# Selective scan on VectorE and GpSimd: decays of GpSimd's units in SBUF instead of PSUM, and later loads of delta

## The chip, the cores and the metric

The kernel runs on one core of a Trainium2 chip. The metric is the device time of one execution in microseconds (us). Three executions of the kernel before took 2348.87, 2349.60 and 2352.06 us; the median is 2349.6 us. In this text VectorE is DVE, GpSimd is POOL, ScalarE is ACT, TensorE is PE, and SP is the engine whose queue starts most of the DMAs, as in the profile.

## What is computed

The reference is one block of a vision model on an input of 4 x 32 x 32 x 384: a convolutional selective-scan layer, then a linear attention layer and a mixture of 8 experts. The change touches the scan alone. Cut to what matters:

```python
def step(h, inp):                       # over L = 1024 positions
    u_t, d_t, B_t, C_t = inp
    dA = jnp.exp(d_t[..., None] * As)   # the decay
    h = h * dA + (d_t * u_t)[..., None] * B_t[:, :, None, :]
    y = jnp.einsum('bkcn,bkn->bkc', h, C_t)
    return (h, y)
```

There are K = 4 directions, 192 channels and N = 16 states for each of 4 images. Two images and 64 channels of each fill the 128 partitions, and a pair of directions that are each other's reversal is taken in one tile.

## The kernel before, in words

The scan stage has NQ = 12 tiles of UN = 32 units; a unit is one state of one direction, 128 partitions x 1024 positions in f32, and the first 16 units of a tile (a half) run forward, the last 16 backward. For every unit five things are done:

- **decay**: ACT computes exp(a x delta) (line 762), and **C copy**: ACT copies the spread row of C from PSUM to SBUF (line 767);
- **input**: delta x u times B. Two units of three are DVE's: PE spreads the row of B over the partitions into a PSUM slot (`B_PS`, two slots; `spread`, line 1040), and DVE multiplies it in place (`input_of`, line 1496). Every third unit (u = 2, 5, ..., 29: `POOL_UNITS`, 10 of a tile) is POOL's: SP loads the row of B, broadcast, from DRAM into a ring of five SBUF buffers `xin` (`b_row`, line 424), and POOL multiplies it there (`make_input`, line 529);
- **scan**: DVE's tensor_tensor_scan of the decay `f` and the input `x` into a ring of eight SBUF buffers `hst` (`scan`, line 1513);
- **read-out**: POOL multiplies two units' `hst` by their C in one instruction of 2048 columns (`read_outs`, line 546);
- **Y**: PE adds the read-outs of a tile in PSUM with an identity matrix (`add_y`, line 1056), LAG = 5 units behind.

Where the operands of a scan lie: a DVE unit's decay is in SBUF (`decay`, two buffers taken in turn) and its input is in PSUM. A POOL unit's decay is written by ACT into the PSUM slot `B_PS[u % 2]`, and its input `xin` is in SBUF. The two PSUM slots are so shared by all 32 units of a tile by the parity of u. A slot or a buffer may be refilled when the scan of its last holder is done: PE waits at line 1075 for the scan of unit U-2, ACT at line 760 for the scan of `held`. The semaphore `sc_ok` counts finished scans and starts at 2.

The order on each engine is written out by hand. DVE goes in groups of three units (line 1517): the inputs of the two DVE units, then three scans, the POOL unit's last. POOL goes in pairs: before the read-out of units u and u+1 it makes the inputs of u+4 and u+5, if they are its own, so its order over six units is input, read-out, read-out, input, read-out. `read_outs` waits for the scans and the C copies of its pair (lines 543 and 544). PE does for each unit the B spread (DVE units), the C spread and a Y add of an earlier unit. SP walks over the units too (line 433): `b_row` of a POOL unit waits for the scan of the unit whose `xin` buffer it takes, five POOL units or 15 units back; and where U % 16 is `FETCH_AT` = 5, from the second half on, SP waits until the whole previous half is scanned (line 437) and then loads delta and delta x u for the half after this one (`load_delta`, lines 395 and 396). What stands behind that wait in SP's queue, the rows of B among it, waits too.

Of the kernel before, what the change touches and what calls it, by code (L numbers as in the profile page):

```python
# [13 lines left out]
B, HW, C, DI, N, R, K = 4, 32, 384, 192, 16, 24, 4  # L14
S = HW * HW
T = B * S
P = 128
CT = C // P
H2 = P // 2
J = DI // H2  # L20
NP = B // 2
# [6 lines left out]
UN = 2 * N  # L28
HALF = S // 2
HALVES = 2 * OJ  # L30
FETCH_AT = 5
RING = 8
DRING = 2
HRING = 8
# [3 lines left out]
XRING = 5  # L38
# [4 lines left out]
MADE = 4  # L43
# [42 lines left out]
def pool_units(u):  # L86
    return u // GROUP


POOL_UNITS = list(range(GROUP - 1, UN, GROUP))  # L90
# [19 lines left out]
    return k, j, p * OJ + o * J + j, dr  # L110


def decay_slot(u):
    return (u - pool_units(u)) % DRING


def decay_before(u):

    vec = [v for v in range(-UN, UN) if v % UN not in POOL_UNITS]
    return vec[vec.index(u) - DRING]  # L120


assert len(POOL_UNITS) % XRING == 0


# [22 lines left out]
def hybrid_block_kernel(nc, a, out):  # L148
    with ExitStack() as ctx:
        def sem(name):  # L150
            return ctx.enter_context(nc.semaphore(name))
# [10 lines left out]
        COLS = 53200  # L162
# [47 lines left out]
        rs = Region(arena, BCD, COLS)  # L210
        xin, decay = rs.take(XRING, S), rs.take(DRING, S)
        c_sb, hst = rs.take(RING, S), rs.take(HRING, S)
        d_diag = Region(arena, COLS - P, COLS).take(P)


# [46 lines left out]
        def pair_of_banks(b):  # L262
            return ps[:, b:b + 2, :].rearrange("p b c -> p (b c)")
# [6 lines left out]
        B_PS = [pair_of_banks(0), pair_of_banks(2)]  # L270
# [24 lines left out]
        ab_ok, dm_st = sem("abs_ready"), [sem(f"delta_stored{i}") for i in range(MADE)]  # L295
# [6 lines left out]
        b_ok, c_ok, c_free, dec_ok = (sem(n) for n in ("b_spread", "c_spread", "c_copied", "decay_ready"))  # L302
        p1_ok, sc_ok, p2_ok, ya_ok, yev_ok = (sem(n) for n in ("input_ready", "scanned", "readout_ready", "y_added", "y_evacuated"))
# [32 lines left out]
        def settled(eng):  # L336


            eng.sem_inc(passed, 1)
# [3 lines left out]
        def _(sp):  # L343
# [50 lines left out]
            def load_delta(q, dr):  # L394
                sp.dma_start(dlt[:, dr], dl_dram[q * 2 + dr]).then_inc(dl_ld[dr], 16)
                sp.dma_start(dux[:, dr], du_dram[q * 2 + dr]).then_inc(du_ld[dr], 16)
# [36 lines left out]
            for U in range(NQ * UN):  # L433
                if U % N == FETCH_AT and N <= U < (2 * NQ - 1) * N:

                    half = U // N + 1
                    sp.wait_ge(sc_ok, U - FETCH_AT + 2)
                    load_delta(half // 2, half % 2)
# [180 lines left out]
        def _(act):  # L619
# [118 lines left out]
            def skip_weights(q):  # L738
                nc.scalar.activation(d_diag, ident, ACT.Identity, scale=d_sum[:, q % OJ, :]).then_inc(diag_ok, 1)

            def evacuate_y(q):
                act.wait_ge(ya_ok, q * UN + (UN + HRING))
                nc.scalar.activation(xy[:, q, :], Y_PS, ACT.Copy).then_inc(yev_ok, 1)

            def units(q, first, last):
                for u in range(UN):
                    dr, n = divmod(u, N)
                    U = q * UN + u
                    if n == 0:

                        act.wait_ge(dl_ld[dr], q * 16 + 16)

                    if u == LAG and not first:
                        evacuate_y(q - 1)
                        skip_weights(q)

                    held = u - 2 if u in POOL_UNITS else decay_before(u)
                    dst = B_PS[u % 2] if u in POOL_UNITS else decay[:, decay_slot(u)]
                    if not (first and held < 0):
                        act.wait_ge(sc_ok, q * UN + (held + 3))  # L760
                        settled(act)
                    nc.scalar.activation(dst, dlt[:, dr], ACT.Exp,  # L762
                                         scale=a_neg[:, q % OJ, dr, n:n + 1]).then_inc(dec_ok, 1)
                    act.wait_ge(c_ok, U + 1)

                    act.wait_ge(p2_ok, U + 1)
                    nc.scalar.activation(c_sb[:, u % RING], C_PS, ACT.Copy).then_inc(c_free, 1)  # L767
# [5 lines left out]
            act.wait_ge(setup, 2)  # L773
            skip_weights(0)
            units(0, True, False)
            with nc.scalar.Fori(1, NQ - 1) as q:
                units(q, False, False)
            units(NQ - 1, False, True)
            evacuate_y(NQ - 1)

# [132 lines left out]
        def _(pe):  # L913
# [122 lines left out]
            def spread(q, u, m, dst):  # L1036

                dr, n = divmod(u, N)
                for h in range(2):
                    mm = pe.matmul(dst[:, h * 512:(h + 1) * 512], sel_lhs[0:BR, n],  # L1040
                                   bc[0:BR, q % OJ // J, dr, m, h * 512:(h + 1) * 512], start=True, stop=True)
                return mm
# [17 lines left out]
            def add_trailing_y(q, u, first):  # L1060
                if u >= LAG:
                    add_y(q, u - LAG)
                elif not first:
                    add_y(q - 1, UN - LAG + u)

            def tile_steps(q, first, last):
                if not first and not last:
                    pe.wait_ge(bc_ld, 16 * ((q + 1) // J + 1))
                for u in range(UN):
                    dr, n = divmod(u, N)  # L1070
                    U = q * UN + u

                    at = u % GROUP
                    if u not in POOL_UNITS:
                        pe.wait_ge(sc_ok, U + 1)
                        spread(q, u, 0, B_PS[u % 2]).then_inc(b_ok, 1)
                    if at == 1:
                        add_trailing_y(q, u - 1, first)
                    pe.wait_ge(c_free, U + 1)
                    spread(q, u, 1, C_PS).then_inc(c_ok, 1)  # L1080
                    if at:
                        add_trailing_y(q, u, first)
# [6 lines left out]
            pe.wait_ge(rows_ok, K * NP)  # L1089
            pe.wait_ge(dtev_ok, NP * HALVES)  # L1090
            tile_steps(0, True, False)
            with nc.tensor.Fori(1, NQ - 1) as q:
                tile_steps(q, False, False)
            tile_steps(NQ - 1, False, True)
            for u in range(UN - LAG, UN):
                add_y(NQ - 1, u)
# [233 lines left out]
        def _(dve):  # L1330
# [156 lines left out]


            def input_of(q, u):
                dr, x = u // N, B_PS[u % 2]  # L1490
                seen = q * VEC_UNITS + (u - pool_units(u) + 1)
                if u % N == 0:

                    dve.wait_ge(du_ld[dr], q * 16 + 16)
                dve.wait_ge(b_ok, seen)
                nc.vector.tensor_tensor(x, x, dux[:, dr], ALU.mult).then_inc(p1_ok, 1)  # L1496

            def scan(q, u):
                dr, U = u // N, q * UN + u
                h, slot = hst[:, u % HRING], B_PS[u % 2]  # L1500
                if u in POOL_UNITS:
                    f, x = slot, xin[:, pool_units(u) % XRING]

                    dve.wait_ge(in_ok, q * len(POOL_UNITS) + (pool_units(u) + 1))
                else:
                    f, x = decay[:, decay_slot(u)], slot

                    dve.wait_ge(p1_ok, q * VEC_UNITS + (u - pool_units(u) + 1))
                dve.wait_ge(dec_ok, U + 1)
                dve.wait_ge(ya_ok, U + 1)  # L1510
                if dr:
                    h, f, x = h[:, ::-1], f[:, ::-1], x[:, ::-1]
                nc.vector.tensor_tensor_scan(h, f, x, 0.0, ALU.mult, ALU.add).then_inc(sc_ok, 1)  # L1513

            def scans(q):

                for g in range(0, UN, GROUP):
                    units = range(g, min(g + GROUP, UN))
                    for u in units:
                        if u not in POOL_UNITS:  # L1520
                            input_of(q, u)
                    for u in units:
                        scan(q, u)
# [367 lines left out]
```

## Time and profile before

| what | value |
|---|---|
| median of three executions | 2349.6 us |
| the profiled execution's own time | 2349.24 us |
| its span in the profile | 2347.4 us |
| busy share of the span: PE, DVE, POOL, ACT | 87%, 67%, 55%, 49% |
| first DVE input of the scan to last POOL read-out | 299.2 to 1481.1 us |
| scans, of which of POOL units | 384, 120 |
| rows of B loaded for POOL units | 240 DMAs of 256 KB, 7.7 us to landing |

The page of the profile gives shares of the whole span; the scan is the middle half of it (slices 6 to 25 of 40). In that part the page shows DVE and POOL at nine tenths and more in nearly every slice, ACT at six to seven and PE at eight. Durations in the profile are those of an instruction on its engine; time in which an engine waits for a semaphore is shown as idle time before an instruction, with what ended it.

### The profile page before, as it was taken

How to read it: one execution, taken by the hardware profiler on the slowest of the kernel's cores; microseconds unless marked ns; L12 is line 12 of the kernel's file. 1: busy time of each engine (PE TensorE's matmuls, PEld its weight loads, DVE VectorE, ACT ScalarE, POOL GpSimd, SP SyncE). 2: the span in 40 equal slices, each digit the busy share in tenths (PEclk: the TensorE clock that was granted, in tenths of full speed). 3: DMA queues.
4: the chain of work that ended last, by engine and by line, in shares of the span. 5: the costliest groups of instructions: out<-in, count | busy, mean ns of one | idle time of the engine just before them, and what ended most of it. 6: DMA issues, size and time to landing. Idle time of an engine off the chain costs nothing.

```text
span 2347.4 us, 20258 instructions
## 1 busy us (share of the span) xinstructions
PE 2031.5 (87%) x5902; PEld 940.8 (40%) x5902; DVE 1577.5 (67%) x1480; ACT 1141.0 (49%) x1238; POOL 1298.9 (55%) x467
## 2 busy tenths in 40 slices
PE   6996668888888888888888888779996899999998
PEld 3432223333333333333333333346553455555554
DVE  5686999999999999999999999472555000000000
ACT  2684866766666666676666767111221221211111
POOL 0101079999999999999999999501223111111110
PEclk9987679999999999999999999889998899999999
DMA  5454533221333223332123220510224433333310
GB/s 211 170 196 134 206 99 102 77 72 54 85 93 86 71 54 85 100 79 71 54 73 98 79 77 22 218 41 1 81 107 142 169 116 121 121 118 121 112 31 7
DMA packets 78850, 231.98 MB, mean 99 GB/s; under 512 B 10783, under 2 KB 37009, under 8 KB 76880
## 3 DMA queue, kind: packets, MB, share of 16 engines
q1 hardware_dynamic: 72656, 214.39, 29.1%
q0 software_dynamic: 6144, 16.98, 2.0%
q8 instruction: 24, 0.39, 0.1%
q14 instruction: 26, 0.21, 0.0%
HBM read 169.24 MB, written 64.03 MB: 99 GB/s over the span
## 4 chain that ended last, share of the span: by engine, by line
PE 46%; DVE 18%; issue 15%; POOL 14%; ACT 5%; DMA 1%; ACTq 0%; DVEq 0%; POOLq 0%; SPq 0%
PE ps L1315 11%; PE ps L1303 11%; DVE arena L1513 10%; POOL arena L546 9%; PE ps L1056 7%; POOL arena L529 5%; PE ps L1251 3%; PE ps L1040 2%; PE ps L955 2%; ACT arena L767 1%; DVE arena L1389 1%; DVE ps L1496 1%; PE ps L1053 1%; PE ps L982 1%; PE ps L1202 1%
## 5 line engine op out<-in xcount | busy, mean ns | idle before, releaser
L546 POOL TENSOR_TENSOR arena<-arena 128x2048 f32<-128x2048 f32 x192 | 865.9, 4523 | 2.9 <-DVE arena L1513 2.9
L1056 PE MATMUL ps<-arena 128*128 128x512 f32 x1536 | 732.5, 599 | 59.9 <-POOL arena L546 59.8
L1513 DVE TENSOR_TENSOR_SCAN arena<-arena,ps 128x1024 f32<-128x1024 f32 x264 | 587.9, 2268 | 0.0
L767 ACT ACTIVATE arena<-ps 128x1024 f32<-128x1024 f32 x384 | 390.9, 1018 | 270.9 <-PE ps L1040 269.4
L1040 PE MATMUL ps<-arena 96*128 (+1 forms) x1296 | 366.6, 387 | 115.0 <-DVE arena L1513 94.0
L1056 PEld LDWEIGHTS ps<-arena 128*128 128x128 f32 x1536 | 287.8, 190 | 324.1 <-issue 193.8
L529 POOL TENSOR_TENSOR arena<-arena 128x1024 f32<-128x1024 f32 x120 | 283.0, 2358 | 128.9 <-DMA arena<-b_rows 128.9
L1496 DVE TENSOR_TENSOR ps<-ps,arena 128x1024 f32<-128x1024 f32 x264 | 309.9, 1219 | 28.5 <-PE ps L1040 28.2
L1793 DVE TENSOR_TENSOR arena<-ps,arena 128x384 f32<-128x384 f32 x32 | 17.8, 558 | 449.2 <-PE ps L1315 449.2
L762 ACT ACTIVATE arena<-arena 128x1024 f32<-128x1024 f32 x264 | 300.8, 1140 | 8.4 <-DVE arena L1513 7.9
L1040 PEld LDWEIGHTS ps<-arena 96*128 96x128 bf16 x1296 | 116.3, 99 | 444.0 <-issue 188.2
L1513 DVE TENSOR_TENSOR_SCAN arena<-ps,arena 128x1024 f32<-128x1024 f32 x120 | 271.9, 2266 | 7.9 <-ACT ps L762 4.2
L605 POOL DMA_INDIRECT out<-arena x32 | 31.7, 992 | 436.1 <-DVE arena L1798 436.1
L1315 PE MATMUL ps<-arena 128*128 128x384 f32 x768 | 250.1, 486 | 0.0
L1303 PE MATMUL ps<-arena 128*128 128x512 f32 x576 | 249.0, 593 | 0.0
L1315 PEld LDWEIGHTS ps<-arena 128*128 128x128 f32 x768 | 145.4, 190 | 101.6 <-issue 3.8
L762 ACT ACTIVATE ps<-arena 128x1024 f32<-128x1024 f32 x120 | 134.1, 1117 | 83.8 <-DVE arena L1513 83.8
L1303 PEld LDWEIGHTS ps<-arena 128*128 128x128 f32 x576 | 109.6, 191 | 136.1 <-issue 133.7
L891 ACT ACTIVATE arena<-ps,arena 128x512 f32<-128x512 f32 x96 | 66.0, 688 | 176.3 <-PE ps L1303 176.3
L578 POOL TENSOR_TENSOR arena<-arena 128x384 f32<-128x384 f32 x32 | 27.0, 878 | 203.2 <-DVE arena L1635 203.2
L898 ACT ACTIVATE arena<-arena 128x384 f32<-128x384 f32 x32 | 16.7, 523 | 232.0 <-DVE arena L1793 232.0
L517 POOL COPY arena<-arena 128x1024 f32<-128x1024 f32 x6 | 13.3, 2217 | 190.2 <-ACT arena L648 190.2
(202 smaller groups left out, 1668.0 us busy)
## 6 DMA issues: line engine op xcount, KB each, us to landing
arena<-b_rows SPq DMA_DIRECT2D x240, 256.0 KB, 7.7
arena<-in_w SPq DMA_DIRECT2D x16, 2304.0 KB, 13.3
delta<-arena SPq DMA_DIRECT2D x24, 512.0 KB, 2.9
delta_x<-arena SPq DMA_DIRECT2D x24, 512.0 KB, 3.5
arena<-delta SPq DMA_DIRECT2D x24, 512.0 KB, 3.6
arena<-delta_x SPq DMA_DIRECT2D x24, 512.0 KB, 4.6
arena<-in_xT SPq DMA_DIRECT2D x6, 1536.0 KB, 9.7
slot_in<-arena SPq DMA_DIRECT2D x8, 772.0 KB, 14.0
```

Of the source, the lines that this page charges most:

```text
L529: nc.gpsimd.tensor_tensor(xin[:, x % XRING], xin[:, x % XRING], dux[:, dr], ALU.mult).then_inc(in_ok, 1)
L546: nc.gpsimd.tensor_tensor(hst[:, h:h + 2], hst[:, h:h + 2], c_sb[:, c:c + 2], ALU.mult).then_inc(p2_ok, 2)
L762: nc.scalar.activation(dst, dlt[:, dr], ACT.Exp, scale=a_neg[:, q % OJ, dr, n:n + 1]).then_inc(dec_ok, 1)
L767: nc.scalar.activation(c_sb[:, u % RING], C_PS, ACT.Copy).then_inc(c_free, 1)
L891: nc.scalar.activation(h_sb[:, m], ps[:, 3 + m % 3, :], ACT.Gelu_apprx_tanh, bias=b1_col[:, e, m:m + 1]).then_inc(hg_ok, 1)
L1040: mm = pe.matmul(dst[:, h * 512:(h + 1) * 512], sel_lhs[0:BR, n], bc[0:BR, q % OJ // J, dr, m, h * 512:(h + 1) * 512], start=True, stop=True)
L1056: mm = pe.matmul(Y_PS[:, h * 512:(h + 1) * 512], ident, hst[:, u % HRING, h * 512:(h + 1) * 512], start=False, stop=(u == UN - 1))
L1251: mm = pe.matmul(ps[:, attend_bank(i), 0:CA], xnT[:, b % 2, t, i * P:(i + 1) * P], w_eff[:, t], start=(t == 0), stop=(t == CT - 1))
L1303: mm = pe.matmul(ps[:, 3 + m % 3, :], w1[s][:, t, m * P:(m + 1) * P], xeT[:, s, t], start=(t == 0), stop=(t == CT - 1))
L1315: mm = pe.matmul(ps[:, 6 + i % 2, 0:C], h_sb[:, m, i * P:(i + 1) * P], w2[s][:, m], start=(m == 0), stop=(m == MT - 1))
L1496: nc.vector.tensor_tensor(x, x, dux[:, dr], ALU.mult).then_inc(p1_ok, 1)
L1513: nc.vector.tensor_tensor_scan(h, f, x, 0.0, ALU.mult, ALU.add).then_inc(sc_ok, 1)
```

## The change

Three edits. First, the decays of POOL's units go to two new SBUF buffers `decay_p`, taken in turn, and no longer to PSUM; they may be refilled after the scan of the POOL unit two before. The two PSUM slots are taken in turn by DVE's units alone, and PE's B spread waits for the scan of the DVE unit two before, no longer for that of the unit two before. Second, the new buffers lie where the layer before keeps delta, so ACT waits before its first decay of a POOL unit until those stores are done. Third, `FETCH_AT` goes from 5 to 11: SP loads the next delta at another place of its queue.

```diff
-FETCH_AT = 5
+FETCH_AT = 11
...
-def decay_slot(u):
-    return (u - pool_units(u)) % DRING
-
-
-def decay_before(u):
-
-    vec = [v for v in range(-UN, UN) if v % UN not in POOL_UNITS]
-    return vec[vec.index(u) - DRING]
+def turn_of(u):
+
+    return pool_units(u) if u in POOL_UNITS else u - pool_units(u)
+
+
+def two_before(u):
+
+    kind = [v for v in range(-UN, UN) if (v % UN in POOL_UNITS) == (u in POOL_UNITS)]
+    return kind[kind.index(u) - 2]
...
+        decay_p = rs.take(2, S)
+        assert rs.at <= COLS - P - J * C - P
...
-                    held = u - 2 if u in POOL_UNITS else decay_before(u)
-                    dst = B_PS[u % 2] if u in POOL_UNITS else decay[:, decay_slot(u)]
+                    if first and u == POOL_UNITS[0]:
+                        for i in range(MADE):
+                            act.wait_ge(dm_st[i], NP * HALVES // MADE * 32)
+                    held = two_before(u)
+                    dst = (decay_p if u in POOL_UNITS else decay)[:, turn_of(u) % 2]
...
                     if u not in POOL_UNITS:
-                        pe.wait_ge(sc_ok, U + 1)
-                        spread(q, u, 0, B_PS[u % 2]).then_inc(b_ok, 1)
+                        if not (first and two_before(u) < 0):
+                            pe.wait_ge(sc_ok, q * UN + (two_before(u) + 3))
+                        spread(q, u, 0, B_PS[turn_of(u) % 2]).then_inc(b_ok, 1)
...
             def input_of(q, u):
-                dr, x = u // N, B_PS[u % 2]
+                dr, x = u // N, B_PS[turn_of(u) % 2]
...
-                h, slot = hst[:, u % HRING], B_PS[u % 2]
+                h = hst[:, u % HRING]
                 if u in POOL_UNITS:
-                    f, x = slot, xin[:, pool_units(u) % XRING]
+                    f, x = decay_p[:, turn_of(u) % 2], xin[:, pool_units(u) % XRING]
...
-                    f, x = decay[:, decay_slot(u)], slot
+                    f, x = decay[:, turn_of(u) % 2], B_PS[turn_of(u) % 2]
```

## Rows read from the trace of the kernel before

**Rows 1.** Busy time of the engines in the scan stage.

```profile
core 0: us, PE busy (x) PEld busy (x) DVE busy (x) ACT busy (x) POOL busy (x), PEclk, DMA share, GB/s
299.20:1481.10 1181.90, 1010.91 (x2866) 410.70 (x2866) 1140.87 (x649) 802.97 (x788) 1140.45 (x312) 0.98 0.28 75
```

**Rows 2.** The page's costliest groups, those of the scan stage.

```profile
L546 POOL TENSOR_TENSOR arena<-arena 128x2048 f32<-128x2048 f32 x192 | 865.9, 4523 | 2.9 <-DVE arena L1513 2.9
...
L1513 DVE TENSOR_TENSOR_SCAN arena<-arena,ps 128x1024 f32<-128x1024 f32 x264 | 587.9, 2268 | 0.0
...
L529 POOL TENSOR_TENSOR arena<-arena 128x1024 f32<-128x1024 f32 x120 | 283.0, 2358 | 128.9 <-DMA arena<-b_rows 128.9
L1496 DVE TENSOR_TENSOR ps<-ps,arena 128x1024 f32<-128x1024 f32 x264 | 309.9, 1219 | 28.5 <-PE ps L1040 28.2
...
L762 ACT ACTIVATE arena<-arena 128x1024 f32<-128x1024 f32 x264 | 300.8, 1140 | 8.4 <-DVE arena L1513 7.9
...
L1513 DVE TENSOR_TENSOR_SCAN arena<-ps,arena 128x1024 f32<-128x1024 f32 x120 | 271.9, 2266 | 7.9 <-ACT ps L762 4.2
...
L762 ACT ACTIVATE ps<-arena 128x1024 f32<-128x1024 f32 x120 | 134.1, 1117 | 83.8 <-DVE arena L1513 83.8
```

**Rows 3.** Who waited for whom, 299 to 1487 us: total us, times, longest.

```profile
POOL arena L529 <- DMA arena<-b_rows: 128.9, 12, 98.2
PE ps L1040 <- DVE arena L1513: 94.0, 87, 3.8
...
DVE ps L1496 <- PE ps L1040: 28.2, 33, 2.1
...
POOL arena L546 <- DVE arena L1513: 2.9, 3, 1.8
```

**Rows 4.** Timeline of DVE, one group of three units: start, us.

```profile
621.60 2.26 DVE L1513 TENSOR_TENSOR_SCAN arena<-ps,arena 128x1024 f32<-128x1024 f32 x1
623.78 2.34 DVE L1496 TENSOR_TENSOR ps<-ps,arena 128x1024 f32<-128x1024 f32 x2
...
630.40 2.26 DVE L1513 TENSOR_TENSOR_SCAN arena<-ps,arena 128x1024 f32<-128x1024 f32 x1
```

**Rows 5.** Timeline of POOL beside it.

```profile
622.65 2.35 POOL L529 TENSOR_TENSOR arena<-arena 128x1024 f32<-128x1024 f32 x1
624.97 9.00 POOL L546 TENSOR_TENSOR arena<-arena 128x2048 f32<-128x2048 f32 x2
```

**Rows 6.** Timeline of SP's queue and of POOL at a half's start.

```profile
398.88 0.33 SPq L395 DMA_DIRECT2D arena<-delta  x1
...
407.63 2.37 POOL L529 TENSOR_TENSOR arena<-arena 128x1024 f32<-128x1024 f32 x1 [2.22 <-DMA arena<-b_rows]
```

**Rows 7.** Durations of single lines: ns min/median/max, first and last start.

```profile
L1513 DVE TENSOR_TENSOR_SCAN arena<-arena,ps x264: 2252/2266/2279, 301.5 to 1474.2; 128x1024 f32<-128x1024 f32 x132
L1513 DVE TENSOR_TENSOR_SCAN arena<-ps,arena x120: 2255/2265/2291, 309.3 to 1465.6; 128x1024 f32<-128x1024 f32 x120
...
L1389 DVE SCALAR_TENSOR_TENSOR arena<-arena x24: 1283/1285/2843, 50.0 to 203.0; 128x1024 f32<-128x1024 f32 x24
...
L1701 DVE TENSOR_TENSOR_SCAN arena<-arena x4: 292/414/641, 1672.0 to 1808.5; 128x64 f32<-128x64 f32 x4
```

**Rows 8.** Timeline of POOL and DVE in the layer before the scan.

```profile
70.09 5.25 DVE L1389 SCALAR_TENSOR_TENSOR arena<-arena 128x1024 f32<-128x1024 f32 x4
...
188.79 6.81 DVE L1389 SCALAR_TENSOR_TENSOR arena<-arena 128x1024 f32<-128x1024 f32 x4
...
189.31 2.56 POOL L517 COPY arena<-arena 128x1024 f32<-128x1024 f32 x1 [107.19 <-ACT arena L648]
...
206.80 1.99 POOL L517 COPY arena<-arena 128x1024 f32<-128x1024 f32 x1 [6.20 <-ACT arena L648]
```

**Rows 9.** Timeline of POOL and DVE in the attention layer.

```profile
1671.24 6.83 POOL L578 TENSOR_TENSOR arena<-arena 128x384 f32<-128x384 f32 x8 [46.32 <-DVE arena L1635]
...
1673.16 0.84 DVE L1704 TENSOR_TENSOR arena<-arena 128x64 f32<-128x64 f32 x1
...
1808.99 0.23 DVE L1704 TENSOR_TENSOR arena<-arena 128x64 f32<-128x64 f32 x1
```

More of the change, by code:

```diff
@@ L110, in half_of @@
     return k, j, p * OJ + o * J + j, dr
-def decay_slot(u):
-    return (u - pool_units(u)) % DRING
-def decay_before(u):
-    vec = [v for v in range(-UN, UN) if v % UN not in POOL_UNITS]
-    return vec[vec.index(u) - DRING]
+def turn_of(u):
[3 more added lines that the diff above has]
+    return kind[kind.index(u) - 2]
+assert len(POOL_UNITS) % 2 == 0
 assert len(POOL_UNITS) % XRING == 0
```

## The prediction

> **What bounds the kernel now.** I read the busy time by stretches first, because the page's shares are taken over stages with different limits. The change lives between 299.2 and 1481.1 us, and there two engines are full: of 1181.9 us DVE is busy 1140.87 and POOL 1140.45, PE 1010.91 and ACT 802.97 [rows 1]. Next the groups, to see what these sums are made of: POOL's are 192 read-outs of 4523 ns and 120 inputs of 2358 ns; DVE's are 384 scans of 2.27 us and 264 inputs of 1219 ns [rows 2]. Instructions of one engine overlap a little, so their sums are above the busy time. Then the waits. POOL's idle time in the stage is 128.9 us for rows of B, of which the first, 98.2 us, is the wait for the stage to start; 30.7 us lie inside it, 11 times, and 2.9 us more are for scans. DVE waits 28.2 us for B spreads [rows 3]. So both engines have some 30 to 40 us to give back, and neither can give back more, since the other stands at 1140 us right behind it. Where POOL's 30.7 us come from is seen at a half's start: SP issues the delta load at 398.88 us, the rows of B behind it only then, and POOL's input at 407.63 us has waited 2.22 us for its row [rows 6].
>
> How the two engines run beside each other is in the timelines. A full group of three units takes DVE 630.40 - 621.60 = 8.80 us; of these, 630.40 - 623.78 = 6.62 us are the two inputs and the first two scans, and 2.18 us is the POOL unit's scan [rows 4]. POOL needs for six units three read-outs and two inputs; started back to back a read-out takes about 4.49 us (two have 9.00 us, and one alone 4.52) and an input 624.97 - 622.65 = 2.32 us [rows 2, 5]. That is 18.1 us for six units, or 9.05 us a group. POOL is thus the slower one by a hair, 9.05 against 8.80.
>
> **Part 1: decays of POOL's units in SBUF.** What is the same: number and size of all instructions. ACT's 120 decays become writes to SBUF, 1140 instead of 1117 ns, 2.8 us in all on an engine with 379 us to spare [rows 1, 2]: nothing. What is new is that 120 scans have both inputs in SBUF. The stage has no such DVE instruction now: every scan and every input of DVE takes one operand from PSUM. All 384 scans lie between 2252 and 2291 ns though POOL works beside them nearly without a pause [rows 7], so an instruction with one SBUF input is not disturbed by POOL.
>
> Instructions with both inputs in SBUF are found elsewhere. Line 1389 takes about 1285 ns, but one of its 24 took 2843 [rows 7]. It belongs to the four that started at 188.79 and took 6.81 us in place of 5.25, and at 189.31 POOL started a copy [rows 8]. Laid out: the first of the four runs to 188.79 + 1.28 = 190.07; POOL's copy, issued in its midst, ends at 191.87, and took 2.56 us where the same copy alone took 1.99 [rows 8]; the second of the four starts at 190.1, takes 2.84 and ends at 192.9, and if its own work is 1.28 it began to flow at 191.6. So each waited for the other to end: POOL for DVE, then DVE for POOL, one at a time. The same shows where POOL runs 8 instructions of 0.85 us in a row: a DVE tensor_tensor of 64 columns takes 0.84 us there and 0.23 when POOL is silent [rows 9], that is one whole POOL instruction each time, and the small scan of line 1701, two SBUF inputs and the very operation of this change, goes from 292 up to 641 ns [rows 7].
>
> So I take it that a POOL unit's scan and a POOL instruction can't run together. POOL works without a pause, so the scan waits for the POOL instruction under way, and POOL's next one waits for the scan. **The cost on POOL** is the hold h of each of 120 scans. Bounds: the copy above needed 191.87 - 190.07 = 1.80 us after its release against 1.99 alone, so 0.19 us of a start may hide under the hold, and the scan's 2.18 (start to start, rows 4) becomes 2.0; upward the scan's full record of 2.27 and, twice that 0.19 lost at a changeover, 2.65 as the far end. I take 2.19, the scan's spacing, as the start of a POOL instruction behind a scan is nearest to its start behind another instruction: 120 x 2.19 = 263 us; ends 240 and 318.
>
> The Trainium skill, "SBUF — State Buffer", section "Who interferes with whom", says just this of a DVE instruction with two SBUF inputs against a GpSimd one that reads SBUF: the second to come is blocked until the first is done. Its section "A bandwidth-pool intuition that's wrong (but worth ruling out)" puts some 115 ns between DVE's end and the blocked one's restart; by it, as an estimate, h were 2.27 + 0.115 and the sum 286 us, 23 more than mine. No row here shows that gap; the copy speaks for a smaller one.
>
> **Is DVE's waiting hidden?** DVE asks for its turn 6.62 us after the last one. Is POOL then starved? In the meantime POOL does whole instructions. After a scan it does input and read-out (2.32 + 4.49 = 6.81) or read-out and input (the same), and DVE waits 0.2; or two read-outs (8.98), and DVE waits 2.4. At these two or three instructions a turn DVE would get through a group in 9.0 to 11.2 us, while POOL needs 9.05 + 2.19 = 11.24 on average. So DVE runs ahead until it needs an input that POOL has only just made; then POOL has already started the read-out behind it, and DVE waits 0.2 + 4.49. Such a turn has read-out, input, read-out (11.3 us + 2.19), the next has input, read-out (6.8 + 2.19): 22.5 us for two groups, again 11.24 each, and the read-outs in it are of units scanned long before. POOL never runs dry, so DVE's waits cost nothing of their own. PE is busy 1010.91 of 1181.9 and gets a stage a fifth longer.
>
> **Part 2: PSUM slots for DVE's units alone.** PE's B spread for a group's first DVE unit waits for a scan two units earlier than it did. This takes away PE's waits for scans (94.0 us, 87 times) and through them DVE's 28.2 us [rows 3]. It is gone, but POOL is the longer chain: worth 0 on the sum. What is late next is POOL's read-out, for the Y adds and for the scans alike.
>
> **Part 3: FETCH_AT 11.** SP comes to the delta load after two more rows of B, which hang on scans 15 units back and so are free by then; the load itself still goes when the previous half is scanned, and has 15 units, over 40 us, to land. Rows of B for units 5 and 8 of a half are in front of it now. POOL's 11 waits in rows 3 go: -30.7 us. Lower bound of the gain 0, if a slower stage would have hidden them anyway (then they are gone too) or if another DMA is late.
>
> **Part 4: ACT's wait for the stored deltas.** Once, before the decay of unit 2. The last delta is made when DVE turns to the scan at 299.2; unit 2's scan waits for POOL's first input anyhow. 0, at most 3 us.
>
> **The sum**, against the profiled execution's own 2349.24 us (the span is 2347.4; the median 2349.6 is the same within 0.02%): 2349.2 - 30.7 + 263 = 2581.5 us. The stage becomes some 1414 us.
>
> **Rivals.**
> - *POOL is starved as well.* If every one of the 120 scans waits for a whole read-out, DVE's chain sets the pace: 1140.87 + 120 x 4.49 = 1680 us against 1181.9 now, a time of 2847. For it: DVE's wait for the fresh input ends as POOL begins a read-out. Against: after such a turn DVE is late, and the next one costs it 0.2. In every second group only, it is my forecast. Chance 0.08, with anything between 2650 and 2847.
> - *Shared, not exclusive.* The scan takes a column in 2.1 ns and may leave room, so that each side is stretched by a part: half of h, 120 x 1.1 = 132, gives 2349.2 - 30.7 + 132 = 2450.5. Against: 2843 is 1285 and most of a copy, nothing in between. Chance 0.07.
> - *Faster: the scan does not hold POOL up.* The scan is bound by its own recurrence, and where it reads its two streams might not collide; its evidence is four instructions of 64 columns, and POOL's eight in that stretch kept 6.83 / 8 = 0.85 us [rows 9], not visibly held. The place is line 1513's 120 scans, the price is that h is 0, and it decides if their mean stays at 2.27 us. Then POOL gives back its 30.7: 2318.5 us. Against: those DVE instructions were so short that a POOL start could cover them, and the copy was held by a long one. Chance 0.07.
>
> **Numbers.** Forecast 0.78, and its own range goes from 2349.2 - 30.7 + 240 = 2558 to 2349.2 - 0 + 318 = 2667; the far ends together are unlikely. Range 2550 to 2655, which leaves out the two rivals below it and the starved case. A measurement of this kernel can tell about 0.2%, 5 us, from no change. Faster by more: 0.07; within it: 0.01, where part of a hold just eats the 30.7; slower: 0.92.
>
> **What would show it.** Right: line 1513 with both inputs in SBUF has a mean of 4 to 5 us (own 2.27 and a mean wait near 2.2), spread from 2.3 to 6.8; 120 of POOL's 312 instructions are longer by some 2.2; POOL stays busy without a gap from 307 us to the stage's end, near 1715; its waits for rows of B are gone; the other 264 scans keep 2.27. Wrong: those scans at 2.27 us (the faster rival), POOL with long idle times before line 546 (the starved one), or all instructions stretched by a common part (the shared one).

## The result, and the profile after

| what | before | after |
|---|---|---|
| median | 2350.8 us (4 runs) | 2558.6 us (4 runs, 2557.7 to 2561.2) |
| ratio to before | | 1.0883, 95% interval 1.0867 to 1.0899 |
| profiled execution, its span | 2349.24, 2347.4 us | 2561.22, 2559.4 us |

The changed kernel is slower by 8.8%, about 208 us; the forecast was 2581.5 us in a range of 2550 to 2655. First the engines' busy time by stretches, as in [rows 1]: the scan stage of the changed kernel, what comes before it and what comes after it.

```profile
299.20:1693.00 1393.80, 1107.64 (x2867) 448.21 (x2867) 1277.64 (x649) 809.50 (x789) 1376.67 (x312) 0.90 0.23 64
0.00:299.20 299.20, 230.25 (x486) 93.99 (x486) 224.94 (x259) 180.25 (x178) 18.13 (x15) 0.83 0.52 184
1693.00:2559.40 866.40, 791.73 (x2550) 437.59 (x2550) 211.59 (x573) 157.54 (x273) 140.41 (x140) 0.96 0.28 102
```

The stage goes from 1181.9 to 1393.8 us, 211.9 more, and that is all of the difference between the two profiled executions: it still begins at 299.2, and the part behind it is 866.4 us in place of 2347.4 - 1481.1 = 866.3. In the stage POOL's busy time has grown by 1376.67 - 1140.45 = 236.2 us and DVE's by 1277.64 - 1140.87 = 136.8 us, with the same 312 and 649 instructions. Which ones grew, the groups of the stage say (line numbers have moved by 4 to 8; x is the count, behind the bar stand busy us, mean ns of one, and idle time before them with its releaser), to be held against [rows 2]:

```profile
L550 POOL TENSOR_TENSOR arena<-arena 128x2048 f32<-128x2048 f32 x192 | 983.2, 5134 | 9.3 <-DVE arena L1521 8.6 <-ACT arena L774 0.7
...
L1521 DVE TENSOR_TENSOR_SCAN arena<-arena,ps 128x1024 f32<-128x1024 f32 x264 | 587.5, 2265 | 0.0
...
L533 POOL TENSOR_TENSOR arena<-arena 128x1024 f32<-128x1024 f32 x120 | 402.6, 3355 | 98.4 <-DMA arena<-b_rows 98.4
...
L1521 DVE TENSOR_TENSOR_SCAN arena<-arena 128x1024 f32<-128x1024 f32 x120 | 405.1, 3376 | 3.1 <-POOL arena L533 3.1
L1504 DVE TENSOR_TENSOR ps<-ps,arena 128x1024 f32<-128x1024 f32 x264 | 311.9, 1218 | 108.4 <-PE ps L1047 107.6
```

The 264 scans with an input in PSUM and DVE's 264 inputs are what they were. The 120 scans with both inputs in SBUF went from 2266 to 3376 ns, and POOL's read-outs and inputs from 4523 to 5134 and from 2358 to 3355 ns. The durations of the single instructions (min/median/max in ns) show that this is not a common stretch; the two lines below are of the changed kernel's scans, the next two of POOL's instructions:

```profile
L1521 DVE TENSOR_TENSOR_SCAN arena<-arena,ps x264: 2251/2266/2278, 301.6 to 1686.0; 128x1024 f32<-128x1024 f32 x132
L1521 DVE TENSOR_TENSOR_SCAN arena<-arena x120: 2255/2280/8447, 309.1 to 1676.6; 128x1024 f32<-128x1024 f32 x120
```

```profile
L550 POOL TENSOR_TENSOR arena<-arena x192: 4493/4529/6551, 313.5 to 1688.4; 128x2048 f32<-128x2048 f32 x192
L533 POOL TENSOR_TENSOR arena<-arena x120: 2344/3304/4386, 306.7 to 1667.8; 128x1024 f32<-128x1024 f32 x120
```

Counted one by one in the trace, 61 of the 120 scans are as short as ever (2.29 us at most), and 59 last 2.46 us and more: they hold a wait inside their record, where it isn't shown as idle time. Of POOL's 312 instructions 119 are longer, each by about 2.0 us, and none lies in between: 60 inputs of 4.22 to 4.39 us beside 60 of 2.34 to 2.38, and 59 read-outs of 6.49 to 6.55 us beside 133 of 4.49 to 4.56. Two groups of three units in the timelines of POOL and of DVE (start, us) show who waits for whom:

```profile
735.73 2.36 POOL L533 TENSOR_TENSOR arena<-arena 128x1024 f32<-128x1024 f32 x1
738.06 4.52 POOL L550 TENSOR_TENSOR arena<-arena 128x2048 f32<-128x2048 f32 x1
742.54 4.35 POOL L533 TENSOR_TENSOR arena<-arena 128x1024 f32<-128x1024 f32 x1
```

```profile
729.19 2.26 DVE L1521 TENSOR_TENSOR_SCAN arena<-arena 128x1024 f32<-128x1024 f32 x1
733.48 2.36 DVE L1504 TENSOR_TENSOR ps<-ps,arena 128x1024 f32<-128x1024 f32 x2 [2.04 <-PE ps L1047]
735.75 4.45 DVE L1521 TENSOR_TENSOR_SCAN arena<-arena,ps 128x1024 f32<-128x1024 f32 x2
740.13 4.60 DVE L1521 TENSOR_TENSOR_SCAN arena<-arena 128x1024 f32<-128x1024 f32 x1
```

At 740.13 the record of a POOL unit's scan begins on DVE; POOL's read-out of 738.06 is in the midst of its 4.5 us and ends at 742.54; the scan's record ends at 744.73, which is 2.2 us, its own length, after that. POOL's next instruction, the input of 742.54, takes 4.35 in place of 2.35 us: it waited 2.0 us for the scan. The two engines take turns, as the prediction read out of the copy in [rows 8]. What the prediction had otherwise is the pace of DVE: before the group of 733.48 DVE stood idle for 2.04 us for a B spread. The waits of the stage (who for whom, total us, times, longest), against [rows 3]:

```profile
PE ps L1063 <- POOL arena L550: 237.0, 92, 4.5
...
DVE ps L1504 <- PE ps L1047: 107.6, 67, 2.6
POOL arena L533 <- DMA arena<-b_rows: 98.4, 2, 98.1
...
PE ps L1047 <- DVE arena L1521: 32.1, 27, 2.2
...
POOL arena L550 <- DVE arena L1521: 8.6, 5, 6.8
```

POOL's waits for rows of B are gone but for the stage's start, PE's waits for scans fell from 94.0 to 32.1 us, and in their place PE waits 237.0 us for read-outs, where the kernel before has this line:

```profile
PE ps L1056 <- POOL arena L546: 59.8, 47, 1.8
```

DVE waits 107.6 us for B spreads that stand in PE's queue behind the Y adds of those read-outs. POOL itself waits 9.3 us for others in 1394, 6.8 of them once (the last section has that case): it is the bound.

### The profile page after: what moved, and what is told of

Same layout as the page of the kernel before. It is cut to its first block, busy times and chain, and to the rows that moved or that the text cites. A ratio compares the mean times of both kernels' runs of the same rounds, so it can differ in the third digit from the quotient of the medians.

```text
span 2559.4 us, 20267 instructions
## 1 busy us (share of the span) xinstructions
PE 2129.6 (83%) x5902; PEld 979.8 (38%) x5902; DVE 1714.2 (67%) x1480; ACT 1147.3 (45%) x1238; POOL 1535.2 (60%) x467
## 4 chain that ended last, share of the span: by engine, by line
PE 38%; POOL 22%; issue 22%; DVE 13%; ACT 2%; DMA 1%; POOLq 0%; DVEq 0%; SPq 0%; ACTq 0%
POOL arena L550 13%; PE ps L1323 10%; PE ps L1311 10%; POOL arena L533 9%; DVE arena L1521 5%; PE ps L1063 4%; PE ps L1259 3%; PE ps L962 2%; PE ps L1047 1%; PE ps L989 1%; DVE ps L1504 1%; DVE arena L1397 1%; PE ps L1210 1%; PE ps L1248 1%; PE ps L1188 1%
## 5 line engine op out<-in xcount | busy, mean ns | idle before, releaser
L1063 PE MATMUL ps<-arena 128*128 128x512 f32 x1536 | 812.2, 655 | 237.5 <-POOL arena L550 237.0
L550 POOL TENSOR_TENSOR arena<-arena 128x2048 f32<-128x2048 f32 x192 | 983.2, 5134 | 9.3 <-DVE arena L1521 8.6
L1063 PEld LDWEIGHTS ps<-arena 128*128 128x128 f32 x1536 | 306.0, 205 | 547.7 <-POOL arena L550 292.4
L769 ACT ACTIVATE arena<-arena 128x1024 f32<-128x1024 f32 x384 | 438.3, 1141 | 78.5 <-DVE arena L1521 76.5
L533 POOL TENSOR_TENSOR arena<-arena 128x1024 f32<-128x1024 f32 x120 | 402.6, 3355 | 98.4 <-DMA arena<-b_rows 98.4
L1047 PE MATMUL ps<-arena 96*128 (+1 forms) x1296 | 384.8, 414 | 52.6 <-DVE arena L1521 32.1
L1521 DVE TENSOR_TENSOR_SCAN arena<-arena 128x1024 f32<-128x1024 f32 x120 | 405.1, 3376 | 3.1 <-POOL arena L533 3.1
L1504 DVE TENSOR_TENSOR ps<-ps,arena 128x1024 f32<-128x1024 f32 x264 | 311.9, 1218 | 108.4 <-PE ps L1047 107.6
L1047 PEld LDWEIGHTS ps<-arena 96*128 96x128 bf16 x1296 | 135.5, 107 | 394.7 <-issue 259.3
L1311 PE MATMUL ps<-arena 128*128 128x512 f32 x576 | 249.0, 594 | 0.0
L1323 PEld LDWEIGHTS ps<-arena 128*128 128x128 f32 x768 | 145.7, 191 | 101.3 <-issue 3.8
L1311 PEld LDWEIGHTS ps<-arena 128*128 128x128 f32 x576 | 110.0, 191 | 135.8 <-issue 133.4
L962 PE MATMUL ps<-arena 128*128 128x512 f32 x144 | 69.2, 635 | 3.0 <-DVE arena L1382 2.6
```

The lines of the kernel that those rows point to most:

```text
L533: nc.gpsimd.tensor_tensor(xin[:, x % XRING], xin[:, x % XRING], dux[:, dr], ALU.mult).then_inc(in_ok, 1)
L550: nc.gpsimd.tensor_tensor(hst[:, h:h + 2], hst[:, h:h + 2], c_sb[:, c:c + 2], ALU.mult).then_inc(p2_ok, 2)
L769: nc.scalar.activation(dst, dlt[:, dr], ACT.Exp, scale=a_neg[:, q % OJ, dr, n:n + 1]).then_inc(dec_ok, 1)
L962: mm = pe.matmul(slot[:, h * 512:(h + 1) * 512], w_in[:, t, r, j], xt[:, r, t, h * 512:(h + 1) * 512], start=(t == 0), stop=(t == CT - 1))
L1063: mm = pe.matmul(Y_PS[:, h * 512:(h + 1) * 512], ident, hst[:, u % HRING, h * 512:(h + 1) * 512], start=False, stop=(u == UN - 1))
L1311: mm = pe.matmul(ps[:, 3 + m % 3, :], w1[s][:, t, m * P:(m + 1) * P], xeT[:, s, t], start=(t == 0), stop=(t == CT - 1))
```

## The experiments

Theory A is the prediction's: a DVE scan with two SBUF inputs and a POOL instruction exclude each other, and POOL, busy from end to end, pays. Rival B: the time comes from the new order of waits (the PSUM slots, PE's queue) or from ACT's writes to SBUF. Open besides was what the move of the delta loads gives, alone and in the changed kernel. The kernel before, timed beside the runs, had a median of 2353.6 us in experiments 1 to 4 and 2352.1 in 5 and 6, against 2350.8 beside the changed kernel; differences between kernels of different sets are uncertain by some 3 us for that alone.

**1. One SBUF input, the rest as changed.** The scan of a POOL unit takes its second operand from a PSUM slot; buffers, decays, waits and POOL's work stay.

```diff
                 if u in POOL_UNITS:
                     f, x = decay_p[:, turn_of(u) % 2], xin[:, pool_units(u) % XRING]
+                    if True:
+                        x = B_PS[turn_of(u - 1) % 2]
```

and PE's B spread into that slot waits for this scan too, so the slots aren't DVE's units' alone here.

> The changed kernel, but the scan of a POOL unit takes its second operand from the PSUM slot of the DVE unit before it, not from xin (POOL still makes xin, and the scan still waits for it); the decays stay in SBUF. Left out: the POOL units' own input in the recurrence. PE's B spread into that slot waits for one scan more. Theory A (a DVE scan with two SBUF inputs and a POOL instruction exclude each other, POOL is the bound): the 120 scans go back to 2.27 us, POOL's two groups to 4523 and 2358 ns, and the time is the prediction's sum without the hold, 2318 us (2315 to 2335). Rival B (the time comes from the new order of waits, PE's B spreads behind Y adds behind read-outs, or from the decays' writes to SBUF): nothing of that is changed here, so about 2559 us stays.

Measured: 2333.1 us, ratio to before 0.9913 (0.9895 to 0.9930). The groups of the stage:

```profile
L557 POOL TENSOR_TENSOR arena<-arena 128x2048 f32<-128x2048 f32 x192 | 868.9, 4538 | 15.2 <-DVE arena L1530 14.4
L1530 DVE TENSOR_TENSOR_SCAN arena<-arena,ps 128x1024 f32<-128x1024 f32 x384 | 850.3, 2264 | 8.2 <-ACT arena L776 4.5 <-POOL arena L540 3.3 <-issue 0.4
L1511 DVE TENSOR_TENSOR ps<-ps,arena 128x1024 f32<-128x1024 f32 x264 | 309.2, 1216 | 13.3 <-PE ps L1054 13.0
L540 POOL TENSOR_TENSOR arena<-arena 128x1024 f32<-128x1024 f32 x120 | 283.6, 2363 | 98.5 <-DMA arena<-b_rows 98.4
```

All 384 scans have 2264 ns again and POOL's instructions their old lengths. Rival B falls: its whole order of waits is in this kernel, with one wait more, and ACT's writes to SBUF are too, and it is not slow. The place of one operand costs 2558.6 - 2333.1 = 225.5 us, 1.88 us for each of 120 scans (226.8 between the two profiled executions, 228 by the ratios to the kernel before).

**2. Half of them.** The same for every second POOL unit (`if turn_of(u) % 2`).

> The same edit for every second POOL unit alone, so 60 scans of 384 have two SBUF inputs. Left out: the own input of every second POOL unit. Theory A with POOL as the bound throughout: half of the hold, 60 x 1.97 us = 118 us over the kernel without it, some 2437 us (2425 to 2445). If DVE's waits rather than POOL's were what counts, the cost would be less than half, since DVE has more room for each wait: below 2400 us. Rival B: 2559 us.

Measured: 2452.3 us, ratio 1.0419 (1.0400 to 1.0439). The expectation, 2437 in a range of 2425 to 2445, was low by 15 us and missed, because it began at 2318, not at 2333; the step from there, 118 us, was right. Over experiment 1 it is 119.2 us for 60 scans, 1.99 each; the other 60 add 106.3, or 1.77 each.

```profile
L557 POOL TENSOR_TENSOR arena<-arena 128x2048 f32<-128x2048 f32 x192 | 902.4, 4711 | 18.0 <-DVE arena L1530 15.6
...
L540 POOL TENSOR_TENSOR arena<-arena 128x1024 f32<-128x1024 f32 x120 | 365.2, 3043 | 99.4 <-DMA arena<-b_rows 99.4
```

In POOL's own records the two halves cost alike: 902.4 + 365.2 - (868.9 + 283.6) = 115.1 us for the first 60, and 983.2 + 402.6 - (902.4 + 365.2) = 118.2 us for the others. What differs is POOL's idle time before its read-outs: 15.2 us in experiment 1, 18.0 here and 9.3 in the changed kernel. So the holds go with the number of such scans, and the time a little less, because POOL waits less for others.

**3. The kernel before with the loads moved.**

```diff
-FETCH_AT = 5
+FETCH_AT = 11
```

> The kernel before with FETCH_AT = 11 and nothing else. By the prediction's part 3 POOL's 11 waits for rows of B (30.7 us) go and POOL, at 9.05 us a group, stays the bound: 2318.5 us, up to 2330 if DVE's waits for B spreads (28 us, PSUM slots still shared) take over a part. Rival: the rows arrive later for another reason or the delta loads are late at the next half: no change at 2350.

Measured: 2333.6 us, ratio 0.9914 (0.9896 to 0.9932). This version computes the whole result and beats both kernels; the gain is below 1% but clear of noise. The expectation, 2318.5 and up to 2330, was missed: the gain is 20.0 us by the medians taken side by side (2353.6 to 2333.6) and 14.9 by the profiled executions (2349.24 to 2334.31), half to two thirds of the 30.7. Its groups and two lines of POOL's timeline tell why:

```profile
L546 POOL TENSOR_TENSOR arena<-arena 128x2048 f32<-128x2048 f32 x192 | 867.9, 4531 | 15.8 <-DVE arena L1513 14.9
...
L529 POOL TENSOR_TENSOR arena<-arena 128x1024 f32<-128x1024 f32 x120 | 283.4, 2362 | 98.4 <-DMA arena<-b_rows 98.4
```

```profile
529.93 4.53 POOL L546 TENSOR_TENSOR arena<-arena 128x2048 f32<-128x2048 f32 x1 [1.21 <-DVE arena L1513]
626.33 4.53 POOL L546 TENSOR_TENSOR arena<-arena 128x2048 f32<-128x2048 f32 x1 [1.21 <-DVE arena L1513]
```

The rows' waits in the stage, 30.7 us, are gone, but POOL now waits 14.9 us for scans, where it had waited 2.9 [rows 3]: some 1.2 us in every tile, once in 96.4 us. DVE's pace was too near to POOL's for POOL to take back all of its idle time. Experiment 1 has the same time (2333.1), with the decays in SBUF. But that doesn't price the freed PSUM slots: there a POOL unit's scan reads such a slot too, and PE waits 121.8 us for scans against 112.3 here. No run has the slots for DVE's units alone without the collision.

**4. The changed kernel with the loads where they were** (`FETCH_AT` back to 5).

> The changed kernel with FETCH_AT = 5. If part 3's 30.7 us are gained in the changed kernel too, this is slower by as much, 2589 us. Rival: with the holds DVE's scans run further ahead of POOL's read-outs, so that SP gets past its wait early enough for the rows of B anyway; then the waits for rows are near 0 here as well and the time is that of the changed kernel, 2559 us within 5.

Measured: 2561.8 us, ratio 1.0890 (1.0871 to 1.0910); the changed kernel had 1.0883 (1.0867 to 1.0899), so no difference is shown. The rival had the time right and its reason wrong: the waits for rows are there.

```profile
L550 POOL TENSOR_TENSOR arena<-arena 128x2048 f32<-128x2048 f32 x192 | 985.0, 5144 | 1.5 <-DVE arena L1521 1.5
...
L533 POOL TENSOR_TENSOR arena<-arena 128x1024 f32<-128x1024 f32 x120 | 382.4, 3187 | 122.9 <-DMA arena<-b_rows 122.9
```

POOL waits 122.9 us for rows, 24.5 more than the changed kernel's 98.4. But its instructions sum to 985.0 + 382.4 = 1367.4 us against 983.2 + 402.6 = 1385.8, 18.4 less, and it waits 7.8 us less for others at the read-outs (1.5 in place of 9.3). The timelines of DVE and POOL show how the shorter instructions come about:

```profile
540.70 2.27 DVE L1521 TENSOR_TENSOR_SCAN arena<-arena 128x1024 f32<-128x1024 f32 x1
```

```profile
535.94 4.54 POOL L550 TENSOR_TENSOR arena<-arena 128x2048 f32<-128x2048 f32 x1
542.50 2.63 POOL L533 TENSOR_TENSOR arena<-arena 128x1024 f32<-128x1024 f32 x1 [2.02 <-DMA arena<-b_rows]
```

POOL waits for its row from 540.48 to 542.50, and the scan with two SBUF inputs lies at 540.70 to 542.97, just there. It holds POOL up by 0.3 us (2.63 against 2.35), not by 2.0. POOL's waits for rows gave some scans room; take the waits away, and the same time comes back, by the sums above mostly as holds (18.4 us) and for the rest as waits for others (7.8).

**5. A shorter scan.** From the second tile on the POOL units' scans run over 512 columns.

```diff
+                if u in POOL_UNITS and not (isinstance(q, int) and q == 0):
+                    h, f, x = h[:, 0:HALF], f[:, 0:HALF], x[:, 0:HALF]
```

> The changed kernel; from the second tile on, the scan of a POOL unit runs over the first 512 of its 1024 columns (110 scans; left out: the other half of those units' recurrence, POOL still reads it out). The hold as the scan's own length less a start hidden under it: a scan of 512 columns is some 1.07 us shorter, so a hold is 1.97 - 1.07 = 0.9 us, and over the kernel with one SBUF input (2333 us) the cost is 10 x 1.97 + 110 x 0.9 = 119 us: 2452 us (2440 to 2460); POOL's lengthened instructions are longer by 0.9 us. Rival, a fixed price of a changeover of some 2 us whatever the scan's length: the time stays near 2559 us.

Measured: 2442.6 us, ratio 1.0400 (1.0376 to 1.0424).

```profile
L550 POOL TENSOR_TENSOR arena<-arena 128x2048 f32<-128x2048 f32 x192 | 926.9, 4840 | 4.5 <-DVE arena L1523 4.5
...
L533 POOL TENSOR_TENSOR arena<-arena 128x1024 f32<-128x1024 f32 x120 | 343.8, 2865 | 98.2 <-DMA arena<-b_rows 98.2
```

```profile
898.54 4.54 POOL L550 TENSOR_TENSOR arena<-arena 128x2048 f32<-128x2048 f32 x1
903.05 3.28 POOL L533 TENSOR_TENSOR arena<-arena 128x1024 f32<-128x1024 f32 x1
```

POOL's instructions are longer than in experiment 1 by (926.9 + 343.8) - (868.9 + 283.6) = 118.2 us, expected 119; the held input takes 3.28 us, 0.93 above its 2.35. In the trace 110 of POOL's instructions are longer by 0.92 us and 10 by 2.0, as many as there are short and long scans. A short scan that doesn't wait takes 1.19 us and a long one 2.27, so at both lengths a hold is the scan less 0.27 us, and there is no fixed price. The time came out nearer to the lower end of its range, 109.5 us over experiment 1 in place of 119, because POOL waits 4.5 us before its read-outs where it waited 15.2 there.

**6. Two such scans in a group.** The second DVE unit of each group scans `xin` too.

```diff
                     dve.wait_ge(p1_ok, q * VEC_UNITS + (u - pool_units(u) + 1))
+                    if u % GROUP == 1 and u + 1 < UN:
+                        x = xin[:, pool_units(u + 1) % XRING]
+                        dve.wait_ge(in_ok, q * len(POOL_UNITS) + (pool_units(u + 1) + 1))
```

> The changed kernel, but the second DVE unit of each group of three scans xin of its group's POOL unit in place of its own PSUM input, so 240 scans have two SBUF inputs, the two of a group one behind the other (left out: the own input of those 120 units; their scan also waits for POOL's input of the group). If POOL and DVE take turns, a POOL instruction runs between the two, and each costs POOL its 1.97 us: 2333 + 240 x 1.97 = 2806 us or more, more because DVE now waits twice in a group (8.80 + two waits of up to 4.5 us against POOL's 9.05 + 3.94 = 13.0). If instead DVE keeps the port for two scans in a row, POOL is held up once, by 4.45 - 0.2 = 4.2 us: about the same sum, 2333 + 120 x 4.2 = 2837, but then POOL's instructions show single holds of 4.2 us and the second scan no wait.

Measured: 2806.3 us, ratio 1.1935 (1.1915 to 1.1954). The timelines of POOL and DVE over one group:

```profile
900.86 4.50 POOL L550 TENSOR_TENSOR arena<-arena 128x2048 f32<-128x2048 f32 x1
905.31 4.34 POOL L533 TENSOR_TENSOR arena<-arena 128x1024 f32<-128x1024 f32 x1
909.62 6.51 POOL L550 TENSOR_TENSOR arena<-arena 128x2048 f32<-128x2048 f32 x1
```

```profile
903.10 8.70 DVE L1524 TENSOR_TENSOR_SCAN arena<-arena 128x1024 f32<-128x1024 f32 x2
```

The two scans take 8.70 us in place of 4.45, and between them POOL gets a turn: the input of 905.31 is held for 2.0 us and the read-out of 909.62 for another 2.0. So the engines take turns instruction by instruction; the longest of POOL's inputs and read-outs are 4.35 and 6.52 us, so there is no hold of 4.2 us. That the sum was met to the microsecond (2806) is luck: POOL's instructions grew by 1091.5 + 494.8 - 1152.5 = 433.8 us over experiment 1, less than the 240 x 1.97 = 473 of the sum, and only 227 of the 312 are longer; and POOL waited 47.4 us for scans (63 times, against 14.4 us in experiment 1), since DVE, waiting twice a group, now falls behind at times. This is the starved case of the rivals, begun.

## Why the prediction was right, point by point

- **What bounds the stage**: right. POOL was busy 1376.67 of 1393.8 us.
- **Part 1, the mechanism**: right, and shown by experiments 1, 2 and 5: the cost appears with the second SBUF input, goes with the count, and follows the scan's length. With the exclusion that the Trainium skill states ("SBUF — State Buffer", "Who interferes with whom") the trace agrees: 2.0 us held on POOL, 2.3 us waited on DVE at 740.13. The one scan of the last section waited for more than the instruction under way, which neither I nor the rule as I told it had. One reading was loose: the instruction of 64 columns that took 0.84 us in place of 0.23 waited 0.61 us, which is less than one whole POOL instruction of 0.85 [rows 9].
- **Part 1, the size of the hold**: the term that was mis-sized. I took 2.19 us, the scan's spacing; measured is 2.0 us, 119 times, or 236.2 / 120 = 1.97 us for each scan. The lower bound, 2.0, drawn from the 0.19 us that the copy had hidden [rows 8], was the value; it should have been taken, being the row nearest to a POOL instruction released by DVE. In time the hold cost 225.5 us against the 263 of the sum, 37.5 less: 26.8 by the size and most of the rest since POOL waits for others less than in experiment 1 (9.3 against 15.2 us) and its instructions there were already 3.6 us longer in sum than before (1152.5 against 1148.9). The estimate by the Trainium skill ("SBUF — State Buffer", "A bandwidth-pool intuition that's wrong (but worth ruling out)"), with 115 ns between DVE's end and the restart and 286 us, is further off; the section gives that figure for a DMA that waits for its descriptors, and here a held POOL instruction is longer by the scan's length less 0.27 us.
- **DVE's waiting is hidden**: right in the result (POOL waits 9.3 us for others), wrong in the picture. I had DVE stopped by inputs that POOL had only just made and then made to wait for a whole read-out, 4.49 us in every second group. About every second scan waits (59 of 120), but mostly for what is left of a read-out. DVE is stopped one step earlier, by B spreads behind Y adds (107.6 us, 67 times), and its wait in the scans is 3376 - 2266 = 1.11 us in the mean, not 2.2. The forecast of 4 to 5 us for those scans was too long.
- **Part 2, PSUM slots**: worth 0 was forecast, for the reason that POOL is the longer chain. It fits that POOL waits 9.3 us in all, but no run has the freed slots by themselves, so it is argued and not shown. That PE's 94.0 us of waits for scans and DVE's 28.2 us of waits for B spreads would go was wrong in the changed kernel: PE kept 32.1, and DVE's became 107.6, for another reason. And within a group the B spread waits for a scan one unit earlier than before (u-3 in place of u-2), not two.
- **Part 3, the loads**: the waits went as said, but not the time. Alone the move gains 15 to 20 us of the 30.7 (experiment 3), as DVE was next; in the changed kernel it gains nothing that can be told, since those waits had covered holds.
- **Part 4**: 0, as said: POOL's first input starts at 306.7 us, where it was at 306.9 before.
- **The sum**: 2349.2 - 30.7 + 263 = 2581.5 was forecast, 232.3 us more. In the two profiles POOL's busy time in the stage grew by 236.2 us and its idle time fell from 41.4 (1181.9 - 1140.45) to 17.1 us (1393.8 - 1376.67), by 24.3: 236.2 - 24.3 = 211.9. The two misses, 26.8 us on the hold and 6.4 on the idle time, are of opposite sign, so some of the nearness is their cancelling; the range did not need it, for with the hold alone put right the sum is 2554.7. The split between hold and loads depends on the order in which they are taken: with `FETCH_AT` left at 5 the collision costs 2561.8 - 2353.6 = 208.2 us, and the move then gains nothing (experiment 4). The faster rival asked for holds of 0 and the shared one for half; neither is left by 119 holds of 2.0 us each with nothing in between.

## What to carry to other kernels

Where DVE and POOL are both full, look at where each DVE operand lies before moving one out of PSUM: a second SBUF input makes a long DVE instruction and POOL's work take turns, and nearly the whole length of it (2.0 of 2.27 us, 0.92 of 1.19) is added to POOL's chain. An operand kept in PSUM, even in a slot that others wait for, was worth some 225 us here. And the idle time of an engine that such holds fall on is not free to be won: removed by rows that came in time it came back, mostly as holds, while in the kernel without them the same one-line move gained 0.9%.

## What the hardware showed that was not expected

One scan took 8447 ns. The timelines of POOL and DVE about it:

```profile
764.64 4.52 POOL L550 TENSOR_TENSOR arena<-arena 128x2048 f32<-128x2048 f32 x1
769.12 2.35 POOL L533 TENSOR_TENSOR arena<-arena 128x1024 f32<-128x1024 f32 x1
771.44 4.52 POOL L550 TENSOR_TENSOR arena<-arena 128x2048 f32<-128x2048 f32 x1
782.77 4.52 POOL L550 TENSOR_TENSOR arena<-arena 128x2048 f32<-128x2048 f32 x1 [6.81 <-DVE arena L1521]
```

```profile
769.66 8.45 DVE L1521 TENSOR_TENSOR_SCAN arena<-arena 128x1024 f32<-128x1024 f32 x1
```

Its record begins at 769.66, 0.54 us after POOL's input had begun, and ends at 778.11, 2.15 us after the end of the read-out of 771.44: POOL's input and the read-out behind it both ran before it. So a waiting engine was passed over; POOL then ran dry for 6.81 us. It came once more, in experiment 2, again with a POOL input just begun (at 603.90) and again with 6.81 us of idle time on POOL behind it:

```profile
604.33 8.60 DVE L1530 TENSOR_TENSOR_SCAN arena<-arena 128x1024 f32<-128x1024 f32 x1
```

Five other scans of the changed kernel began 0.24 to 0.82 us into an input too and got their turn at its end. Why these two did not stays open.

PE's granted clock in the stage fell from 0.98 [rows 1] to 0.90. In the timeline of PE a wait for a read-out is followed by slow matmuls:

```profile
702.44 0.60 PE L1047 MATMUL ps<-arena 96*128 x2
707.26 3.78 PE L1063 MATMUL ps<-arena 128*128 128x512 f32 x4 [4.22 <-POOL arena L550]
...
713.06 1.88 PE L1063 MATMUL ps<-arena 128*128 128x512 f32 x4
```

And in stretches of 4 us (same columns as [rows 1]; the clock is the third number from the end):

```profile
748.00:752.00 4.00, 0.58 (x1) 0.50 (x2) 4.00 (x3) 1.41 (x2) 4.00 (x2) 0.78 0.00 0
752.00:756.00 4.00, 4.00 (x7) 1.28 (x6) 1.52 (x1) 0.00 (x0) 4.00 (x1) 0.50 0.00 0
```

PE had been busy 0.58 of 4 us, and in the next 4 the clock stood at the lower of its two levels, 1.2 GHz. At that level four matmuls that otherwise take 1.88 us take about twice that, as at 707.26 (3.78 us). This should lengthen DVE's waits for B spreads, but with POOL as the bound I see no time in it: POOL waited 9.3 us for all others together. No run tried it by itself.
